# Three transfers in flight instead of eight: GpSimd's scatters of the edges and gathers of the source terms in a four-layer graph network

## The reference

```
xl     = (x @ W).reshape(n, H, C)                 # H = 4 in layer 0, 8 in layer 2
a_src  = einsum('nhc,hc->nh', xl, att_src)        # one term per node and head
a_dst  = einsum('nhc,hc->nh', xl, att_dst)
logits = leaky_relu(a_src[src] + a_dst[dst], 0.2) # per edge
alpha  = softmax of logits over the edges of one target
out    = segment_sum(xl[src] * alpha, dst)
```

## Time and profile before

| | |
|---|---|
| time, median of 3 runs | 7612.53 us (7604.48 to 7619.08) |
| span of the profiled execution | 8827.0 us |
| TensorE busy | 5772.8 us, 65% of the span |
| VectorE busy | 4203.1 us, 48% |
| GpSimd busy | 4135.2 us, 47% |
| mean granted TensorE clock | 0.767 |
| scatters of the edges (L1714) | 400, busy 420.8 us |
| gathers of source terms (L2266) | 336, busy 321.1 us |

### The profile page before, as it was taken

The page is one execution under the profiler, slowest core; times in us unless marked ns, Lnnn a source line. Parts: engine busy times, 40 slices in busy tenths (PEclk is TensorE's granted clock), DMA queues, the critical chain, the costliest instruction groups (busy, mean ns, idle before and its releaser), DMA issues. The chain is left out here.

```text
span 8827.0 us, 71673 instructions
## 1 busy us (share of the span) xinstructions
PE 5772.8 (65%) x20790; PEld 3543.0 (40%) x20790; DVE 4203.1 (48%) x10631; ACT 1003.1 (11%) x2613; POOL 4135.2 (47%) x4069
## 2 busy tenths in 40 slices
PE   5342526764676666775933767747777777777499
PEld 3231414332563433334721444434444222433387
DVE  7233515667434444445221576676553466344511
ACT  1110100111120000002210012211001000100122
POOL 1664051664346654661644056601763466466133
PEclk9998755786788776556955588868788999655699
DMA  1010112332463332332721133311332566233365
GB/s 51 17 32 12 38 28 94 93 91 61 140 163 93 91 77 80 92 90 77 202 48 32 57 81 89 90 38 44 91 87 63 149 181 180 79 92 91 87 196 172
DMA packets 340393, 787.84 MB, mean 89 GB/s; under 512 B 96775, under 2 KB 197132, under 8 KB 325764
## 3 DMA queue, kind: packets, MB, share of 16 engines
q0 software_dynamic: 213504, 491.66, 22.3%
q1 hardware_dynamic: 126508, 291.60, 9.6%
HBM read 708.94 MB, written 77.24 MB: 89 GB/s over the span
## 5 line engine op out<-in xcount | busy, mean ns | idle before, releaser
L2094 PE MATMUL bank<-arena 128*125 128x256 f32 (+3 forms) x5824 | 2663.4, 567 | 1208.7 <-DMA arena<-TAB,arena 269.6
L2077 POOL DMA_INDIRECT arena<-TAB,arena x2080 | 1996.6, 960 | 1726.9 <-DMA TAB<-arena 706.6
L2094 PEld LDWEIGHTS bank<-arena 128*125 128x125 f32 x5824 | 1200.0, 245 | 2620.4 <-issue 898.2
L2138 DVE TENSOR_TENSOR arena<-bank,arena 125x256 f32 (+3 forms) x2912 | 1352.6, 465 | 1550.0 <-PE bank L2094 990.2
L2077 POOL DMA_INDIRECT arena<-TABa,arena x832 | 861.7, 1036 | 996.3 <-DVEq L138 597.6
L2117 DVE TENSOR_SCALAR arena<-arena 128x125 f32<-128x125 f32 x2080 | 614.5, 296 | 268.6 <-PE bank L2094 115.0
L1714 POOL DMA_INDIRECT REC<-arena x400 | 420.8, 1052 | 421.0 <-DVE arena L1932 301.1
L1319 POOL DMA_INDIRECT SUM<-arena x192 | 307.5, 1602 | 479.8 <-DVE arena L1537 408.2
L337 PE MATMUL bank<-arena 128*125 128x256 f32 (+4 forms) x1600 | 455.7, 433 | 107.4 <-DVE arena L715 37.7
L2266 POOL DMA_INDIRECT arena<-TERMa,arena x336 | 321.1, 956 | 422.6 <-DVEq L138 230.0
L1363 PE MATMUL bank<-arena 128*128 128x256 f32 x2048 | 466.2, 383 | 15.1 <-DVE arena L1525 6.0
(11 more groups left out here) (495 smaller groups left out, 5945.6 us busy)
## 6 DMA issues: line engine op xcount, KB each, us to landing
arena<-L_ffn_pack SPq DMA_DIRECT2D x32, 2054.0 KB
arena<-L_ffn_pack SPq DMA_DIRECT2D x64, 1026.0 KB
arena<-TAB,arena POOLq DMA_INDIRECT x2080
arena<-DLR SPq DMA_DIRECT2D x52, 500.0 KB
arena<-SLR SPq DMA_DIRECT2D x31, 500.0 KB
arena<-TABa,arena POOLq DMA_INDIRECT x832
TAB<-arena SPq DMA_DIRECT2D x20, 625.0 KB
arena<-L_ffn_b SPq DMA_DIRECT2D x96, 128.0 KB
```

Of the source, the lines that this page charges most:

```text
L2077: e.indirect_dma_start(out=m.G[k % RING][:, 0:m.width], out_offset=None, in_=m.table[:, :], in_offset=bass.IndirectOffsetOnAxis(ap=eidx[:, ...
L2094: e.matmul(ps[0:P, 0:m.full], m.S[k % SRING], m.G[k % RING], start=True, stop=True).then_inc(*put("pass_p", m.g, "summed", k))
L2138: e.tensor_tensor(o, banks.of(m.g, "added", k)[0:P, 0:m.full], o, ALU.add).then_inc(*put("pass_v", m.g, "added", k))
```

## The change

Number k waits for the landing of number k - 3 in place of k - 8, for the 400 scatters and for the 144 and 192 gathers. The semaphores, still eight, and the waits at the end stay.

```
@@ prep_pool
-            if b > 7:
-                e.wait_ge(*of("p", "moved", b - 8))
+            if b > 2:
+                e.wait_ge(*of("p", "moved", b - 3))
             e.indirect_dma_start(out=REC[:, :], out_offset=bass.IndirectOffsetOnAxis(ap=ADR[:, b:b + 1], axis=0),
                                  in_=VAL[:, b, :], in_offset=None).then_inc(*land("sort%d" % (b % 8), "p", "moved", b))
@@ logits_pool
-            if k > 16 * a.looks + 7:
-                e.wait_ge(*of(a.g, "term", k - 8))
+            if k > 16 * a.looks + 2:
+                e.wait_ge(*of(a.g, "term", k - 3))
             e.indirect_dma_start(out=a.as_[:, k, :], out_offset=None, in_=a.terms[:, :],
                                  in_offset=bass.IndirectOffsetOnAxis(ap=eidx[:, k:k + 1], axis=0)).then_inc(
                 *land("logit_g%d" % (k % 8), a.g, "term", k))
```

## The result

| | before | after |
|---|---|---|
| time, median | 7612.53 us | 7728.75 us (7713.5 to 7759.43) |
| profiled execution's own time | (not given) | 7759.43 us |
| its span | 8827.0 us | 7757.7 us |
| mean granted TensorE clock | 0.767 | 0.795 |

The account below looks back on a forecast made before the run. No engine was busy over 65%; rebuilt without recording cost, GpSimd was close behind the last engine at three places (slack 27, 24, 25 us). Losses of 13, 50 and 39 us, sum 102, gave 7714 us, range 7604 to 7860.

Parts of the forecast that it names:

- likeliest case: Whole kernel: slower because GpSimd waits for landings beside SP's loads, 7670 to 7790 us, chance 0.48.
- The mechanism: Scatters and gathers: pace becomes the larger of today's and a third of start-to-landing time, about 2.0 us beside SP's loads.
- Sorting: Scatters: GpSimd loses 40 us in 123 us of loads, ends at 761, past the others' 748 by 13 us; slack 27.
- Layer 0: Layer 0's logits: gathers at 2.0 us beside loads, last landed at 1337, 50 us over 1287; slack 24 us.
- Layer 2: Layer 2's logits: gathers at a mean pace of 1.673 us, last landed at 4826, 39 us over 4787; slack 25 us.
- The scatter's unknown landing: Sorting: no row showed it; taken as 3.95 us from SP's plain write, a pace of 1.32 us, under 1.352.
- rival of slow scatters: Sorting: small writes land after 5.6 us everywhere, 186 + 89 = 275 us lost, 7888 us; chance 0.13.
- No change: Rival, whole kernel: landings stay under 3.8 us in the logits too, time stays 7612 us; chance 0.25.
- Faster: Rival, logits: fewer queued gathers let `STR` land sooner, VectorE's waits shrink, at most 24 + 25 us, 7563 us; chance 0.04.
- The prediction's first inference: Sorting and both logits stages: about 700 us of late-starting instructions on other engines is the profiler's recording cost, supported by 1214.5 us.
- slower small transfers may shorten the creeping: Changed kernel's trace: slower small transfers may reduce other engines' late instruction starts and the span; no size given.

Follow-up runs that it names:

- h4_quiet_three: Whole change (three in flight), the logits' SP loads left out after the third piece, against the kernel before: 7638.77 us (one run), before 7608.43 us.
- the clean trace: Trace of the kernel before, unchanged, run again where other engines' instructions do not start late one by one: 7610.3 us, ratio 1.0002, span 7612.1 us.
- h3_gathers_three: Only the 336 gathers with three in flight, scatters with eight, against the kernel before on a chip at 7608.43 us: 7672.95 us, ratio 1.0089.
- the first session's chip: Chip that ran the kernel before unchanged, each half of the change, and four in flight; the kernel before took 8755.24 us, its unchanged copy 8751.13 us.
- e3_gathers_three: Only the 336 gathers with three in flight, scatters with eight, against the kernel before on a chip at 8755.24 us: 8441.36 us, ratio 0.9634.

## Why the prediction was right, and where its terms were not

Forecast 7714 us, range 7604 to 7860, measured 7728.75; likeliest case (slower, by the forecast's mechanism) as predicted. Its sum was 102 us in place of 116, from three terms of which one was far too small and two too large. That the sum comes so near is in part luck: the errors are +41 in the sorting and -20 and -6 in the logits.

**The mechanism** held at each step that the prediction named: idle time before L2266 with a DMA as its releaser, the same before L1714 beside L1740 and L2216, none in quiet stretches. For the logits h4_quiet_three shows it, where the loads are left out; for the sorting it rests on the places of the waits.

**Sorting: 13 predicted, 53.8 measured. This step failed**, at its slack. The delay was about right: 40 predicted, 53.8 measured. The others were right too: addresses were to be ready at 514 and are at 506.2 (the last L1932 in the clean trace), the others were to meet at 748, and VectorE's wait of 32.3 us before 770.19 puts them at 738. What was wrong is GpSimd: I took 1.352 us a scatter from the earlier trace rows and had it done at 721. In the clean trace the last scatter starts at 761.3, (761.3 - 176.2) / 399 = 1.466 us a scatter, because its preparation adds up to 464.4 us in place of 420.8. The median of one is the same (967 and 971 ns); more of them are long. So I rebuilt everyone's stage without the creeping except GpSimd's, whose duration I took over from the creeping trace as if it didn't depend on the others.

The two traces show what the long ones lie beside. The timeline of the clean trace:

```profile
546.14 6.82 DVE L450 TENSOR_TENSOR arena<-arena 125x6400 f32<-125x6400 f32 x1
546.79 7.00 POOL L1714 DMA_INDIRECT REC<-arena  x1 [0.30 <-issue]
552.99 6.82 DVE L452 TENSOR_TENSOR arena<-arena 125x6400 f32<-125x6400 f32 x1
554.10 6.55 POOL L1714 DMA_INDIRECT REC<-arena  x1 [0.30 <-issue]
```

Each preparation ends 0.8 us behind the VectorE instruction that it overlaps. All ten scatters of more than 3 us in the clean trace end within 0.9 us of such an instruction: these two, and eight beside an L1899 of 4.8 us. In the trace there are four, all beside an L1899; L450 starts only at 861.3 us there, behind the last scatter (848.2). Beyond 0.967 us each, the scatters beside L1899 add up to 29.4 us in the clean trace and 14.7 in the other, those beside L450 and L452 to 11.6 and 0, those beside VectorE's L486 to L488 to 13.0 and 0: 39.3 of the 43.6 us. The creeping had kept these instructions apart from the scatters. That VectorE's instruction is what holds the preparation up is read from this coincidence; no run moved one of them.

**Layer 0: 50 predicted, 30.0 measured.** The slack was right: 24 predicted; 216.4 - (984.6 - 798.4) less some 3 us of landing is 27. The delay was too large: 74 us predicted (1334 in place of 1260), 243.0 - 186.2 = 56.8 measured (h3_gathers_three and the clean trace). The pace was to be 2.0 us beside loads, from the 5.9 and 6.2 us of the earlier trace rows, which carry rows of 1 KB; it is 1.70 over the whole stage, with a median landing of 5.0 in the changed kernel.

**Layer 2: 39 predicted, 32.8 measured.** Slack 25 predicted, about 22 measured; delay 65 (4823 in place of 4758) and 298.5 - 243.9 = 54.6.

**The scatter's unknown landing**, taken as 3.95 us, is 2.1 us at the median in the changed kernel and 8.8 at most. The rival of slow scatters falls; in the quiet last third of the sorting only one scatter waits, 0.51 us.

**The rivals.** "No change" rested on landings under 3.8 us beside the loads, or a pace of 1.41; the median landing is 5.0 and the pace 1.70. Its rule of the Trainium skill, the DMA: Bandwidth & Descriptors fixed cost of about 2.0 us (Anatomy of one DMA — SWDGE (gpsimd) path), fits the quiet landings, 2.1 to 2.4 us, and not those beside the broadcast loads, 5.0 at the median. "Faster" needed `STR` to land sooner: VectorE's waits for it are 129.1 us in the changed kernel and 133.0 in the clean trace before, so fewer gathers in flight do next to nothing for them.

**What was taken for the cost of recording.** The prediction's first inference, that the creeping of the earlier trace rows is made by the profiler, is not borne out: on the first session's chip the timed runs are as long as the profiled one (8751.13 and a span of 8766.1 us), and on the others neither creeps. The trace may come from such a chip and its timed runs from another; no chip is on record for them. Whether the creeping belongs to a chip or to something around it stays open. (Layer 2's creeping is 5015.83 - 4787 = 229 us and not 227; nothing rests on it.) Rebuilding the stages without it was right for the 7612 us case all the same. The prediction also said that slower small transfers may shorten the creeping; e3_gathers_three shows that they do, by 314 us.

## What to carry to other kernels

Before limiting how many small indirect transfers are in flight, find the longest landing beside the other queue's large loads, not the mean one, and compare number x pace with it; and then set the delay against the slack of the stage; here four gathers in flight were free only because 26.5 us fitted into 27, and three cost 0.9%. Read who is last at each meeting point from a trace whose span agrees with the timed runs; if there is only one that doesn't, distrust every engine's durations in it, those of the engine that seems untouched too: when the others move, it meets other instructions. And check the partition count of broadcast loads: 128 in place of 125 gave 0.4% here, where none of the depths gained anything.

## What the runs showed of the hardware that was not expected

- The same kernel takes 7608 to 7619 us on two chips and 8755 us on a third; an unchanged copy came within 0.06% of it on the last and within 0.02% on one of the others. The difference is in stages with many small indirect transfers, where other engines' instructions start one by one, every 2.8 us, for TensorE's products. On that chip three gathers in flight in place of eight gain 3.7% and four gain 1.0 and 2.4 us in the two logits stages (1.278 us a gather), while in the sorting three and four gain 69 and 71 us.
- The preparation of a scatter on GpSimd is not constant: 420.8 us for 400 in a creeping trace, 464.4 in a clean one, with single ones of 7.0 us against a median of 0.967, and each one above 3 us ends less than 1 us behind an instruction of VectorE of 4.8 to 6.8 us that it overlaps.
- Padding the broadcast loads to 128 partitions makes a full set of loads 1152 KB in place of 1100 and still raised the rate beside layer 0's gathers from 118 to 132 GB/s (from 104 to 246 before layer 2's gathers begin) and halved VectorE's waits for `STR` (133.0 to 61.8 us).
